# Sparse cross-attention: the smaller halves come from integer sums on GpSimd, and one Relu with a GpSimd minimum replaces two Relu passes

## The reference

```python
Q = _split_heads(x @ Wq.T + bq, N_HEADS)
K = _split_heads(knowledge_embeddings @ Wk.T + bk, N_HEADS)
V = _split_heads(knowledge_embeddings @ Wv.T + bv, N_HEADS)
scores = jnp.einsum('bhsd,bhnd->bhsn', Q, K) / SCALE
topk_scores, topk_indices = jax.lax.top_k(scores, 32)
sparse_weights = jax.nn.softmax(topk_scores, axis=-1)
sel_V = jnp.take_along_axis(V[:, :, None, :, :], topk_indices[..., None], axis=3)
context = jnp.einsum('bhsk,bhskd->bhsd', sparse_weights, sel_V)
```

## Time and profile before

| engine | busy in the program, us | share | busy in 200 us of the changed stage, us |
|---|---|---|---|
| PE | 3490.1 | 80% | 153.26 |
| DVE | 3360.0 | 77% | 196.39 |
| ACT | 2818.1 | 65% | 192.67 |
| POOL (GpSimd) | 1017.5 | 23% | 83.33 |

### The profile page before, as it was taken

One profiled execution on the slowest core, in us unless ns is written; L12 is line 12 of the kernel. 1 busy time (PEld: TensorE's weight loads), 2 busy tenths in 40 slices (PEclk: granted clock), 3 DMA queues, 4 the chain that ended last, 5 costly groups with the idle time before them and its releaser, 6 DMA issues. The chain is left out here.

```text
span 4342.4 us, 70861 instructions
## 1 busy us (share of the span) xinstructions
PE 3490.1 (80%) x25855; PEld 2819.6 (65%) x25855; DVE 3360.0 (77%) x5326; ACT 2818.1 (65%) x4654; POOL 1017.5 (23%) x929
## 2 busy tenths in 40 slices
PE   6445749999999788999999975777777777777787
PEld 3334337999999566899999852555555555555676
DVE  4675877777777633877778656999999999999744
ACT  3112616666666443666666542999999999999932
POOL 0000503111220201121112010434444444444310
PEclk9555869999999888999999987999999999999998
DMA  8743011111110021111111001000000000000000
GB/s 270 114 59 109 4 41 39 39 31 39 34 37 16 23 66 36 31 39 31 31 39 31 9 20 41 16 16 16 16 31 16 16 16 18 29 16 8 1 23 18
DMA packets 186341, 161.29 MB, mean 37 GB/s; under 512 B 7996, under 2 KB 174092, under 8 KB 185996
## 3 DMA queue, kind: packets, MB, share of 16 engines
q1 hardware_dynamic: 182604, 142.83, 12.5%
q10 hardware_dynamic: 3392, 13.93, 0.9%
HBM read 127.36 MB, written 20.20 MB: 34 GB/s over the span
## 5 line engine op out<-in xcount | busy, mean ns | idle before, releaser
L559 PEld LDWEIGHTS psU<-ctxN,ST 128*128 128x128 f32 x6656 | 853.7, 191 | 98.4 <-issue 39.7
L559 PE MATMUL psU<-ctxN,ST 128*128 128x129 f32 x6656 | 868.1, 275 | 20.7 <-issue 20.7
L1174 DVE MAX8 top<-pairs 128x8 f32<-128x801 f32 (+1 forms) x512 | 702.8, 1398 | 0.1
L1136 POOL TENSOR_TENSOR P<-P,EX 128x1601 f32<-128x1601 f32 x128 | 460.4, 3597 | 705.8 <-ACT P L1051 705.8
L645 ACT ACTIVATE ST<-ST 128x512 f32<-128x512 f32 (+1 forms) x832 | 513.2, 625 | 167.1 <-DVE ST L747 163.1
L945 PE MATMUL psU<-ctxN,PT 128*128 128x129 f32 (+1 forms) x3328 | 429.9, 280 | 200.6 <-ACT PT L1059 200.6
L747 DVE TENSOR_TENSOR ST<-ST,psB 128x512 f32<-128x512 f32 (+1 forms) x832 | 556.2, 677 | 3.4 <-PE psB L578 3.4
L733 DVE TENSOR_TENSOR psA<-psA,ST 128x512 f32<-128x512 f32 x640 | 446.6, 698 | 137.4 <-ACT ST L637 69.4
L945 PEld LDWEIGHTS psU<-ctxN,PT 128*128 128x128 f32 (+1 forms) x3328 | 393.0, 192 | 224.8 <-ACT PT L1059 224.7
L1184 DVE MATCH_REPLACE8 pairs<-top,pairs 128x801 f32<-128x801 f32 (+1 forms) x384 | 480.1, 1255 | 0.0
L547 PE MATMUL psS<-statL,ctxH 128*128 128x512 f32 x832 | 393.6, 473 | 5.7 <-ACT ST L637 2.7
(11 more groups left out here) (505 smaller groups left out, 6216.5 us busy)
## 6 DMA issues: line engine op xcount, KB each, us to landing
ctxN<-in_ctx SPq DMA_DIRECT2D x48, 768.0 KB
ahead_ctxT<-ctxT_scratch SPq DMA_DIRECT2D x32, 800.5 KB, 4.4
ctxT_scratch<-trn ACTq DMA_DIRECT2D x16, 800.5 KB
ctxT<-ctxT_scratch SPq DMA_DIRECT2D x16, 800.5 KB, 6.1
nat<-in_ctx SPq DMA_DIRECT2D x16, 768.0 KB
dist_scratch<-dd SPq DMA_DIRECT2D x8, 800.5 KB
skewed<-in_ctx SPq DMA_DIRECT2D x8, 768.0 KB
ctx_late<-in_ctx SPq DMA_DIRECT2D x8, 768.0 KB
```

Source lines behind the costliest of these rows:

```text
L559: last = pe.matmul(psU[:, q, 0:D + 1], ST[0:n, i % SLOTS, q * 128:q * 128 + 128], ctxN[0:n, j, k, 0:D + 1], start=(k == 0 and q % 2 == 0), ...
L1136: pool.tensor_tensor(P[:, j, :], P[:, j, :], EX[:, j, :], ALU.mult).then_inc(p_ready, 1)
L1174: dve.max(top_t[:, 8 * n:8 * n + 8], pairs_t[:, 0:HALF if n < 2 else KP]).then_inc(listed_early if n < 2 else listed_late, 1)
```

## The change

The two folds of a tile are split between engines. DVE makes only the larger halves, now into a tile `maxes` of their own. GpSimd reads both halves of the scores as 32-bit integers, adds them (`add_halves`), and later subtracts the bit patterns of the larger halves (`take_maxes`); what is left is the bit pattern of the smaller ones. `pairs` now has three buffers. The first drop reads `maxes` and writes `pairs`; the third search waits for the smaller halves.

The mark is one Relu of (needed - 1601 x side), where `needed` is the listed sum plus 32, and GpSimd then takes the minimum of that and span before it multiplies. A column above the 32nd is clamped to span, a tie gives needed, one below gives zero. GpSimd's own loop is written out in a new order.

```diff
-        pairs = c.sb(st, "pairs", [128, 2, KP])
+        maxes = c.sb(st, "maxes", [128, 2, HALF])
+        pairs = c.sb(st, "pairs", [128, 3, KP])
...
                         pe.wait_ge(copied, t + ONE)
-                        pe.wait_ge(folded, 2 * t + ONE)
+                        pe.wait_ge(folded, t + ONE)
...
                     if t >= 2:
-                        act.wait_ge(rest_ready, t - 1 + ONE)
+                        act.wait_ge(needed_ready, t - 1 + ONE)
+                        act.wait_ge(spanned, 2 * (t - 1) + ONE)
...
                 def mark(t):
                     j = t % 2
-                    act.wait_ge(rest_ready, t + 1 + ONE)
+                    act.wait_ge(needed_ready, t + 1 + ONE)
...
-                    act.activation(P[:, j, :], sides[:], ACT.Relu, scale=span[:, j:j + 1], bias=rest[:, j:j + 1]
-                                   ).then_inc(graded, 1)
-                    act.wait_ge(graded, t + 1 + ONE)
-                    act.activation(P[:, j, :], P[:, j, :], ACT.Relu, scale=-1.0, bias=span[:, j:j + 1]).then_inc(marked, 1)
+                    act.activation(P[:, j, :], sides[:], ACT.Relu, scale=-float(K), bias=needed[:, j:j + 1]
+                                   ).then_inc(marked, 1)
...
-                def equal_span(t):
+                def add_halves(t):
+                    if t >= 3:
+                        pool.wait_ge(listed_late, LATE * (t - 2) + ONE)
+                    pool.wait_ge(copied, t + 1 + ONE)
+                    pool.tensor_tensor(pairs[:, t % 3, HALF:KP].bitcast(I32), SS[:, t % 3, 0:HALF].bitcast(I32),
+                                       SS[:, t % 3, HALF:KP].bitcast(I32), ALU.add).then_inc(added_up, 1)
+
+                def take_maxes(t):
+                    pool.wait_ge(added_up, t + 1 + ONE)
+                    pool.wait_ge(folded, t + 1 + ONE)
+                    mins = pairs[:, t % 3, HALF:KP].bitcast(I32)
+                    pool.tensor_tensor(mins, mins, maxes[:, t % 2, :].bitcast(I32), ALU.subtract).then_inc(mins_ready, 1)
+
+                def count_equal(t):
...
                     if t >= 2:
                         pool.wait_ge(marked, t - 1 + ONE)
+                        pool.wait_ge(clamped, t - 1 + ONE)
+                    pool.tensor_scalar(needed[:, j:j + 1], above[:, j:j + 1], float(TOPK), None, ALU.add
+                                       ).then_inc(needed_ready, 1)
...
                 def weigh(t):
                     j = t % 2
                     pool.wait_ge(spanned, 2 * t + 2 + ONE)
-                    pool.tensor_scalar(rest[:, j:j + 1], span[:, j:j + 1], -float(TOPK), above[:, j:j + 1],
-                                       ALU.add, ALU.subtract).then_inc(rest_ready, 1)
                     pool.wait_ge(marked, t + 1 + ONE)
+                    pool.tensor_scalar(P[:, j, :], P[:, j, :], span[:, j:j + 1], None, ALU.min).then_inc(clamped, 1)
                     pool.wait_ge(exp_done, t + 1 + ONE)
+                    pool.wait_ge(clamped, t + 1 + ONE)
                     pool.tensor_tensor(P[:, j, :], P[:, j, :], EX[:, j, :], ALU.mult).then_inc(p_ready, 1)
...
-                for s in range(T + 1):
-                    if s >= 1:
-                        equal_span(s - 1)
-                        weigh(s - 1)
+                add_halves(0)
+                for s in range(T + 2):
+                    if s < T:
+                        take_maxes(s)
+                    if s >= 2:
+                        count_equal(s - 2)
+                    if s + 1 < T:
+                        add_halves(s + 1)
+                    if s >= 2:
+                        weigh(s - 2)
...
-                def fold(t, low):
+                def fold(t):
...
-                        dve.wait_ge(listed_late, LATE * (t - 1) + ONE)
-                    if low:
-                        dve.tensor_tensor(pairs[:, j, HALF:KP], lo, hi, ALU.min).then_inc(folded, 1)
-                    else:
-                        dve.tensor_tensor(pairs[:, j, 0:HALF], lo, hi, ALU.max).then_inc(folded, 1)
+                        dve.wait_ge(mins_ready, t - 1 + ONE)
+                        dve.wait_ge(listed_early, EARLY * (t - 2) + 2 + ONE)
+                    dve.tensor_tensor(maxes[:, t % 2, :], psS[:, 0:HALF], SS[:, t % 3, HALF:KP], ALU.max
+                                      ).then_inc(folded, 1)
...
                     elif n == 2:
-                        dve.wait_ge(folded, 2 * t + 2 + ONE)
+                        own = pairs_t
+                        dve.wait_ge(mins_ready, t + 1 + ONE)
...
-                    dve.match_replace(own, top_t[:, 8 * n:8 * n + 8], own, LOW
+                    dve.match_replace(left, top_t[:, 8 * n:8 * n + 8], maxes[:, t % 2, :] if n == 0 else left, LOW
```

More of the change, by code:

```diff
@@ L822, in topk_cross_attention @@
         span = c.sb(st, "span", [128, 2])
-        rest = c.sb(st, "rest", [128, 2])
+        needed = c.sb(st, "needed", [128, 2])
         li = c.sb(st, "li", [128, 2])
@@ L847, in topk_cross_attention @@
         folded, max_ready = c.sem("folded"), c.sem("max_ready")
+        added_up, mins_ready = c.sem("halves_added"), c.sem("mins_ready")
         listed_early, listed_late = c.sem("listed_early"), c.sem("listed_late")
@@ L850, in topk_cross_attention @@
         counted, sided, spanned = c.sem("counted"), c.sem("sided"), c.sem("spanned")
-        rest_ready, graded = c.sem("rest_ready"), c.sem("graded")
+        needed_ready, clamped = c.sem("needed_ready"), c.sem("clamped")
         p_ready, turned, pt_ready = c.sem("p_ready"), c.sem("turned"), c.sem("pt_ready")
@@ L1147, in _ @@
             def _(dve):
-                def fold(t, low):
-                    j = t % 2
-                    lo, hi = psS[:, 0:HALF], SS[:, t % 3, HALF:KP]
+                def fold(t):
                     dve.wait_ge(copied, t + 1 + ONE)
                     if t >= 2:
-                        dve.wait_ge(listed_late, LATE * (t - 1) + ONE)
-                    if low:
-                        dve.tensor_tensor(pairs[:, j, HALF:KP], lo, hi, ALU.min).then_inc(folded, 1)
-                    else:
-                        dve.tensor_tensor(pairs[:, j, 0:HALF], lo, hi, ALU.max).then_inc(folded, 1)
+                        dve.wait_ge(mins_ready, t - 1 + ONE)
+                        dve.wait_ge(listed_early, EARLY * (t - 2) + 2 + ONE)
+                    dve.tensor_tensor(maxes[:, t % 2, :], psS[:, 0:HALF], SS[:, t % 3, HALF:KP], ALU.max
+                                      ).then_inc(folded, 1)
                 def find(t, n):
-                    pairs_t, top_t = pairs[:, t % 2], top[:, t % 3]
+                    pairs_t, top_t = pairs[:, t % 3], top[:, t % 3]
                     if n == 0:
-                        dve.wait_ge(folded, 2 * t + 1 + ONE)
+                        own = maxes[:, t % 2, :]
+                        dve.wait_ge(folded, t + 1 + ONE)
                         if t >= 3:
@@ L1167, in find @@
                     elif n == 1:
+                        own = pairs_t[:, 0:HALF]
                         dve.wait_ge(listed_early, EARLY * t + 2 + ONE)
                     elif n == 2:
-                        dve.wait_ge(folded, 2 * t + 2 + ONE)
+                        own = pairs_t
+                        dve.wait_ge(mins_ready, t + 1 + ONE)
                         dve.wait_ge(listed_early, EARLY * t + 4 + ONE)
                     else:
+                        own = pairs_t
                         dve.wait_ge(listed_late, LATE * t + 2 + ONE)
-                    dve.max(top_t[:, 8 * n:8 * n + 8], pairs_t[:, 0:HALF if n < 2 else KP]
-                            ).then_inc(listed_early if n < 2 else listed_late, 1)
+                    dve.max(top_t[:, 8 * n:8 * n + 8], own).then_inc(listed_early if n < 2 else listed_late, 1)
                 def drop(t, n):
-                    pairs_t, top_t = pairs[:, t % 2], top[:, t % 3]
-                    own = pairs_t[:, 0:HALF if n < 2 else KP]
+                    pairs_t, top_t = pairs[:, t % 3], top[:, t % 3]
+                    left = pairs_t[:, 0:HALF if n < 2 else KP]
                     if n < 2:
@@ L1198, in add @@
                     dve.tensor_tensor(c.x[:, p, :], c.x[:, p, :], psZ[:, 128:256], ALU.add).then_inc(y_added, 1)
-                fold(0, False)
-                fold(0, True)
+                fold(0)
                 for s in range(T + 3):
@@ L1222, in _ @@
                     if s + 1 < T:
-                        fold(s + 1, False)
-                        fold(s + 1, True)
+                        fold(s + 1)
                 inverse(T - 1)
```

## The result

The changed kernel takes 4532.43 us (median of four runs, 4532.0 to 4536.45), the kernel before 4342.02 beside it. The ratio is 1.0435, with an interval of 1.0423 to 1.0448. The forecast of 4217 was wrong in sign. The second rival of the prediction, priced at 4546, is what happened.

What follows compares the result with a forecast made beforehand. DVE and ACT were taken to bound the stage together at 11.07 us a tile. DVE's 9.99, tied by GpSimd's 9.95, plus 0.1 gave 10.08; over 127 tiles that saves 126 us, so 4217, own range 4195 to 4260, full range to 4490.

Steps and rivals of the forecast that it cites:

- Rival 2: GpSimd's minimum costs 4.33 us as the 201-column row says, 12.68 us a tile, 4546 us in all; chance 0.13.
- minimum against a column ... I take 1.60: GpSimd's new 1601-column minimum: rows gave 1.60 or 4.33 us; 1.60 was taken, slot 1.69.
- cold start: The 749 ns GpSimd row at 201 columns was set aside as the first tensor-scalar of the program.
- ACT and DVE as two loops on top of each other: Before the change, ACT 10.99 and DVE 10.89 us a tile; neither alone could give back more than 0.2.
- ACT's ring: ACT's round of copy, values, scores, score copy, copies, mark: 10.72 us, with key copies 10.99; after the change 9.2.
- DVE minus 0.90: Dropping the minimum of the halves takes DVE from 10.89 to 9.99 us a tile.
- GpSimd's tie with DVE: After the change GpSimd's own work is 9.95 us a tile, level with DVE's 9.99.
- Rival 3: GpSimd integer operations take 2.3 us each, 4304, or from 2.45, 4342; chances 0.04 if still faster, 0.04 no change (shared).
- The other new ring: Product, transposes, two weight copies, mark, minimum, product across engines: 9.1 us, below both DVE and GpSimd.
- The point of 2.7 us from which the change loses: A GpSimd minimum longer than 2.7 us would make the changed kernel slower than before.
- Rivals 1, 4 and 5: 1: minimum 3.0 us, 4375, chance 0.13; 4: ACT ring late, 4330 to 4350, shared 0.04; 5: integers through f32, none.

Runs made afterwards that it cites:

- experiments 1 and 2: Kernel before plus a block ahead of its stages where GpSimd alone runs tensor-scalar forms; at 1601 columns single operations took 4.3 us, cheap pairs 1.53 to 1.69.
- experiment 7: Kernel before with the new mark alone, both folds on DVE: 4447.28 us (1.0242) with the plain minimum, 4310.65 us (0.9924) with minimum then maximum.
- experiment 3: Changed kernel with the GpSimd minimum issued as minimum with span, then maximum with 0.0: 4215.03 us, ratio 0.9708.

## Why the prediction was wrong

*The step that failed* is the term "minimum against a column ... I take 1.60". It measured 4.38. The prediction had both ends, 1.60 and 4.33, and the upper was right to 1%. I chose the lower for two reasons and both fell. The 749 ns at 201 columns were put down to a cold start; 724 is the price each time. And the 408 ns of line 347 were read as the same instruction with two operations; line 347 is an add and a multiply, one of the cheap pairs, and says nothing of a single operation, which costs 4.3 at 1601 columns whether it is minimum, multiply or add (experiments 1 and 2). The rule of the Trainium skill cited there (GPSIMD Engine Reference, Engine selection: one-input work roughly at line rate) holds in these runs for the copy and the cheap pairs, 1.52 to 1.69, and not for the others, 4.25 to 5.74. The cast, the third row on that side, is a copy and not a tensor-scalar. The nearest row in kind, an f32 instruction with one operation, stood in the trace and was the better witness.

*The rest of the sum* was right in the main. With the minimum at 1.59 the kernel takes 4215, and the prediction for that case was 4217; 10.05 us a tile against 10.08.
- ACT and DVE as two loops on top of each other: halves alone give nothing (4344), the mark alone gives 32 us in the cheap form (4311), both together 127. So neither could be had alone beyond 0.3 us a tile, where the prediction said 0.2.
- ACT's ring was priced too low. In the kernel before, the score copies stand 10.72 apart in steps without a key copy and 11.29 to 11.67 in the four with one: a key copy of 0.69 lengthens its step by up to 0.95, since PE's transposes wait for it (69.4 us in 60 tiles) and ACT's weight copies for them. The mean is 11.14 and not 10.99, and 11.14 is the whole steady period. So ACT was the bound, and DVE, at 10.87 (experiment 7), stood 0.27 below it. In the changed kernel this ring has slack, so the error did not reach the forecast.
- DVE minus 0.90: the steady distances are 10.87 with both folds (experiment 7) and (3799.39 - 2829.42) / 96 = 10.10 with one (experiment 3), so 0.77 came off. The first search now stands directly behind the fold whose output it reads, and starts 1.02 us after it, where a fold was 0.90. The lines are from the changed kernel. The bound was indeed DVE.

```profile
3412.24 0.98 DVE L1176 TENSOR_TENSOR maxes<-psS,SS 128x801 f32<-128x801 f32 x1
...
3413.26 1.00 DVE L1198 MAX8 top<-maxes 128x8 f32<-128x801 f32 x1
```
- GpSimd's tie with DVE: 186.81 busy against 199.34. Its own work was about 0.3 a tile lower than the sum's 9.95 (12.41 less the 2.79 by which the minimum is shorter is 9.62), since the integer addition took 1.60 and the subtraction 1.79 on average, not 1.89 each. Rival 3, slow integers, is out.
- The other new ring, said to be 9.1 and below both, did not bind with a short minimum (experiments 3 and 7); its length there was not measured. With the real minimum it is 11.75 and would have cost 105 us even without the halves.
- Rival 2's price, 4546 against 4532, is close in part by luck. It had 12.68 a tile; the steady pace is 12.57, with an addition 0.26 shorter and a minimum 0.11 longer, from start to next start, than its terms. But it put 204 us into the loop, where 171 were measured, and nothing into the drain, where 17 were. The point of 2.7 us from which the change loses was not measured by a run.
- Rivals 1, 4 and 5 did not occur.

*The chances* gave this case 0.13. Two rows of another kind, a cast and a pair of operations, stood against one of the right kind; that was nearer to even than 0.66 to 0.26.

## What to carry to other kernels

Before work is moved to an engine that is idle, find the price of exactly that form: the same operation or pair of operations, not only the same engine, type and width; the second operation of one instruction changed it by a factor of 2.7. When two engines are within a few per cent of each other, each half of a change measured alone shows little: here 0 and 32 us, against 127 for both, so a half without gain says little of the whole. And an engine 75% busy can still set the time through a ring, here product, transposes, copies, mark, minimum.

## What was not expected of the hardware

On GpSimd a 1601-column f32 tensor-scalar took 4.25 to 4.38 us with one operation, 1.53 to 1.69 with four pairs of operations, and 5.6 to 5.74 with the other pairs tried; order counts (minimum then maximum 1.60, maximum then minimum 5.61). Adding a maximum made an instruction faster by 2.8 us. The integer tensor-tensor of 801 columns took 1.87 in a block of its own, as the f32 one did, and 1.60 for the addition in the kernel; the subtraction there took 1.60 in every third tile and 1.88 in the others, in step with its three buffers. Why is open, for the pairs as for the integers. The longer subtractions are worth some 0.2 us a tile; with the dear minimum, where GpSimd is the bound, that is part of the time, with the cheap one it is not.
